# A Relu tile on ScalarE, a second query and key stack filled in the preparation, and one F32 product for the gated mixing

## The reference

```python
# layer 0: 16 heads of 16 columns; hidden width 1024
h = layernorm(x + multihead(x, x, x, sa_wq, sa_wk, sa_wv, sa_wo, causal=True), ln1_g, ln1_b)
h = layernorm(h + multihead(h, ctx, ctx, ca_wq, ca_wk, ca_wv, ca_wo, causal=False), ln2_g, ln2_b)
ff = relu(h @ ff_w1.T + ff_b1) @ ff_w2.T + ff_b2
x = layernorm(h + ff, ln3_g, ln3_b)
# layer 1: single-head gated attention over the context
qp, kp, vp = x @ Wq + bq, ctx @ Wk + bk, ctx @ Wv + bv
w = softmax(einsum('bqd,bkd->bqk', qp, kp) / 16)
y = einsum('bqk,bkd->bqd', w, vp)
gate = concatenate((qp, y), -1) @ Wg + bg
out = y * mask[..., None] * sigmoid(gate) + x
```

## Time and profile before

| | us |
|---|---|
| median of 3 runs | 853.6 (849.36 to 855.4) |
| the profiled execution | 848.75 |
| its span, first to last instruction | 846.9 |
| mean granted TensorE clock | 0.970 |

### The profile page before, as it was taken

One profiled execution on the slowest core, in us unless ns is written; L12 is line 12 of the kernel. 1 busy time (PEld: TensorE's weight loads), 2 busy tenths in 40 slices (PEclk: granted clock), 3 DMA queues, 4 the chain that ended last, 5 costly groups with the idle time before them and its releaser, 6 DMA issues.

```text
span 846.9 us, 20003 instructions
## 1 busy us (share of the span) xinstructions
PE 772.9 (91%) x7214; PEld 644.0 (76%) x7232; DVE 637.9 (75%) x1389; ACT 483.3 (57%) x1113; POOL 486.8 (57%) x598
## 2 busy tenths in 40 slices
PE   6998799999999999788899999899999899999795
PEld 5786588788877766555568888788877789889685
DVE  4535577788788898868778888987787679877854
ACT  5432256655565566565776666566656765544442
POOL 2413367776777676554355666566555677666541
PEclk9999999999999999898799999999999999999977
DMA  9675987788677664354322222222200020112122
GB/s 278 165 265 157 177 141 131 149 135 139 110 130 136 102 103 112 75 126 92 69 54 55 55 54 54 55 54 55 54 2 10 2 71 9 32 58 78 56 83 78
DMA packets 105308, 79.63 MB, mean 94 GB/s; under 512 B 43261, under 2 KB 101967, under 8 KB 104947
## 3 DMA queue, kind: packets, MB, share of 16 engines
q1 hardware_dynamic: 101850, 74.17, 41.7%
q10 hardware_dynamic: 3360, 4.18, 1.5%
HBM read 27.03 MB, written 12.97 MB: 47 GB/s over the span
## 4 chain that ended last, share of the span: by engine, by line
PE 61%; DVE 16%; issue 6%; ACT 4%; SPq 2%; DMA 1%; POOL 1%; POOLq 0%; ACTq 0%; DVEq 0%
PE a_misc L89 12%; PE a_pair L89 11%; PE a_s L1041 8%; PE a_s L806 4%; PE a_pair L830 4%; PE a_pair L848 3%; PE a_pair L1002 3%; PE a_s L804 3%; PE a_pair L987 3%; PE a_pair L1140 2%; PE a_s L964 2%; PE a_s L89 2%; DVE c_z L1593 2%; DVE a_nm L1483 2%; PE a_pair L851 1%
## 5 line engine op out<-in xcount | busy, mean ns | idle before, releaser
L1483 DVE TENSOR_REDUCE a_nm<-a_s 128x2 f32<-128x512 f32 (+1 forms) x192 | 127.1, 678 | 50.9 <-PE a_s L806 50.4
L2005 POOL TENSOR_TENSOR c_hidden<-c_hid,c_hidden 128x256 fp32r<-128x256 f32 x128 | 96.0, 750 | 109.6 <-DVE c_hid L1734 109.5
L1207 ACT ACTIVATE a_pT<-a_pair 128x512 f32<-128x512 f32 x192 | 113.6, 597 | 79.3 <-PE a_pair L830 71.6
L1337 ACT ACTIVATE a_pT<-a_pair 77x512 f32<-77x512 f32 x128 | 75.6, 591 | 100.8 <-PE a_pair L987 98.0
L1041 PE MATMUL a_s<-c_w,c_hidden 128*128 128x256 f32 x768 | 117.3, 292 | 0.0
L89 PE MATMUL a_pair<-c_fxh,c_w 128*128 128x256 f32 x512 | 100.9, 289 | 8.6 <-DVE c_hid L1734 8.5
L1912 POOL TENSOR_SCALAR_AFFINE_SELECT a_pT<-a_pT 128x256 f32<-128x256 f32 (+1 forms) x192 | 91.5, 496 | 22.4 <-ACT a_pT L1207 21.9
L1734 DVE TENSOR_SCALAR c_hid<-a_pair,ff_b_col 128x256 f32<-128x256 f32 x128 | 61.4, 479 | 51.0 <-ACT c_hidden L1363 50.6
L1041 PEld LDWEIGHTS a_s<-c_w,c_hidden 128*128 128x128 f32 x768 | 98.6, 190 | 0.6 <-issue 0.4
L89 PEld LDWEIGHTS a_pair<-c_fxh,c_w 128*128 128x128 f32 x512 | 79.1, 191 | 11.5 <-DVE c_hid L1734 11.1
L806 PE MATMUL a_s<-a_sk,a_sq 96*128 96x256 bf16 (+1 forms) x512 | 74.4, 247 | 6.9 <-DMA a_sk<-a_parts 4.4
(11 more groups left out here) (273 smaller groups left out, 2175.2 us busy)
## 6 DMA issues: line engine op xcount, KB each, us to landing
a_sq<-a_parts SPq DMA_DIRECT2D x96, 128.0 KB, 4.4
a_sk<-a_parts SPq DMA_DIRECT2D x96, 128.0 KB, 4.6
a_sq<-c_parts SPq DMA_DIRECT2D x96, 128.0 KB
x<-in_xT SPq DMA_DIRECT2D x16, 256.0 KB, 6.2
res<-in_x SPq DMA_DIRECT2D x16, 256.0 KB, 5.8
out<-g_fin SPq DMA_DIRECT2D x16, 256.0 KB, 2.1
a_sk<-kc_parts SPq DMA_DIRECT2D x96, 38.5 KB
fold_rows<-x_fold ACTq DMA_DIRECT2D x1, 2496.0 KB, 10.0
```

The costliest lines, as they stand in the source:

```text
L1207: nc.scalar.activation(pT[g % NPT][:], stps[g % 2][:], ACT.Exp).then_inc(s_exp, 1)
L1337: nc.scalar.activation(pT[g % NPX][0:SC], st_ps[0:SC, :], ACT.Exp).then_inc(c_exp, 1)
L1483: nc.vector.tensor_reduce(nm[c % 2][:, QT * heads[0] + qt:QT * heads[-1] + qt + 1:QT], sps[g % 2][:].rearrange("p (h k) -> p h k", h=len(h ...
L2005: nc.gpsimd.tensor_tensor(hl(m), hid[n % NHID][:], f32(hh(m)), ALU.subtract).then_inc(c_hl, 1)
```

## The change

- **Relu tile.** `hidden` moves from VectorE to ScalarE and reads the PSUM tile first; it frees the PSUM buffer. `hidden_high` becomes a copy of that SBUF tile to F32R and stands last in ScalarE's slot. `hidden_low` waits for the copy.
- **Second stack.** The stack of sample 1 is filled in the preparation: after the stores of each of the first six token tiles SyncE issues two of its transfers. The main stage starts with the stack of sample 2. The context keys' parts in the preparation now lie in the memory of the second stack and its neighbour, so the first of the new transfers waits until they have been stored.
- **Biases.** The column biases are loaded before the inputs, and the products that need them wait for them alone. The bias row is no longer split.
- **Mixing.** `mix` makes one F32 product for each row tile, of unsplit probabilities (now two buffers) and unsplit values, which are loaded straight to their place. `p_low`, `value_high` and `value_low` are gone. A value load waits for the mixing three samples before.

```diff
-    t.first_stack = [sb(n, [KX, H, S], BF16) for n in ("sq0", "sk0")]
+    t.first_stacks = [[sb(f"{n}{i}", [KX, H, S], BF16) for n in ("sq", "sk")] for i in range(2)]
...
-    parts = sb("parts", [P, 3, B, KT, SC], BF16)
+    parts = nc.alloc_sbuf_tensor_at("x_parts", [P, 3, B, KT, SC], BF16, offset=t.place["a_sq1"])
...
+            for n, v in t.cols.items():
+                sp.dma_start(v[:], a[n + "_col"]).then_inc(biases, 16)
             for i in range(2):
                 sp.dma_start(t.x[i][:], a["xT"][i].rearrange("(k p) s -> p k s", p=P)).then_inc(t.x_loaded[i], 16)
             for n, v in t.rows.items():
                 sp.dma_start(v[:], A(n).partition_broadcast(P)).then_inc(small, 16)
-            for n, v in t.cols.items():
-                sp.dma_start(v[:], a[n + "_col"]).then_inc(small, 16)
...
+            def load_rows(c, rows, term, i):
+                q, k = t.first_stacks[c]
+                sp.dma_start(q[rows].rearrange("r h s -> r (h s)"),
+                             t.parts[c][:, 0, term].rearrange("p k s -> p (k s)")).then_inc(t.stacked[c], 16)
+                sp.dma_start(k[rows].rearrange("r h s -> r (h s)"),
+                             t.parts[c][:, 1, i].rearrange("p k s -> p (k s)")).then_inc(t.stacked[c], 16)
+
             sp.wait_ge(t.s_p3, 1)
             for rows, term, i in stack_rows():
...
+                load_rows(0, rows, term, i)
+            sp.wait_ge(s_rowb, 1)
+            sp.dma_start(d.row, rowf[:]).then_inc(row_stored, 16)
...
                 sp.dma_start(d.vc[i * P:i * P + r], vs[i % NRING][0:r]).then_inc(t.value_stored[i % NRING], 16)
+                if i == 0:
+                    sp.wait_ge(t.s_p3, 2)
+                    sp.wait_ge(k_stored, 16)
+                if i < NTERM:
+                    load_rows(1, *list(stack_rows())[i])
...
-            pe.wait_ge(small, 16 * (len(t.rows) + len(t.cols) + 1 + 2))
+            pe.wait_ge(biases, 16 * (len(t.cols) + 2))
...
-            act.wait_ge(s_rowb, 1)
-            nc.scalar.activation(row[:, 0, :], rowf[:], ACT.Copy).then_inc(s_rowh, 1)
...
-            dve.wait_ge(s_rowh, 1)
-            nc.vector.tensor_tensor(row[:, 1, :], rowf[:], f32(row[:, 0, :]), ALU.subtract).then_inc(s_rowl, 1)
...
-    gvv = [gat(f"vv{i}", [SCE, 2, 2 * D], F32R, *p) for i, p in enumerate((("a_sq0", 0), ("a_sq0", half), ("a_sq1", 0)))]
-    raw_vv = [gat(f"raw_vv{i}", [SC, 2 * D], F32, f"a_pT{i}") for i in range(ND)]
+    gvv = [gat(f"vv{i}", [SCE, 2 * D], F32, *p) for i, p in enumerate((("a_sq0", 0), ("a_sq0", half), ("a_sq1", 0)))]
...
-    pth, ptl = (gat(n, [SCE, QT, P], F32R, "a_xl0", i * 4 * QT * P) for i, n in enumerate(("pth", "ptl")))
+    p_turned = [gat(f"pt{i}", [SCE, QT, P], F32, "a_xl0", i * 4 * QT * P) for i in range(2)]
...
-            for c in range(1, EARLY):
+            for c in range(2, EARLY):
                 load_stacks(c)
...
-                if c == 0:
-                    sp.wait_ge(c_av, 4 * B)
                 if c >= ND:
-                    sp.wait_ge(g_vl, c - ND + 1)
-                sp.dma_start(raw_vv[c % ND][:], d.vv[c * SC:(c + 1) * SC]).then_inc(g_value[c % ND], 16)
+                    sp.wait_ge(g_xo, c - ND + 1)
+                sp.dma_start(gvv[c % ND][0:SC], d.vv[c * SC:(c + 1) * SC]).then_inc(g_value[c % ND], 16)
...
-                pe.wait_ge(g_ptl, c + 1)
-                pe.wait_ge(g_vl, c + 1)
+                pe.wait_ge(g_pth, c + 1)
+                pe.wait_ge(g_value[c % ND], 16 * (c // ND + 1))
                 for qt in range(QT):
-                    for i, (x, y) in enumerate(((0, 0), (1, 0), (0, 1))):
-                        last = mt(xo(c)[:, qt * 2 * D:(qt + 1) * 2 * D], (pth, ptl)[x][:, qt, :], gvv[c % ND][:, y, :], start=False, stop=i == 2,
-                                  skip_group_check=True)
+                    last = mt(xo(c)[:, qt * 2 * D:(qt + 1) * 2 * D], p_turned[c % 2][:, qt, :], gvv[c % ND][:], start=False, stop=True,
+                              skip_group_check=True)
...
+            def hidden(n):
+                c, m = divmod(n, FT)
+                if not real(c):
+                    return
+                act.wait_ge(c_up, n + 1)
+                atleast(act, c_hl, n - NHID + 1)
+                nc.scalar.activation(hid[n % NHID][:], up[n % 2][:, 0:S], ACT.Relu, bias=b1[:, m:m + 1]).then_inc(c_hid, 1)
+
             def hidden_high(n):
...
-                act.wait_ge(c_up, n + 1)
+                act.wait_ge(c_hid, n + 1)
                 atleast(act, c_down, n - FT + 1)
-                nc.scalar.activation(hh(m), up[n % 2][:, 0:S], ACT.Relu, bias=b1[:, m:m + 1]).then_inc(c_hh, 1)
+                nc.scalar.activation(hh(m), hid[n % NHID][:], ACT.Copy).then_inc(c_hh, 1)
...
-            def p_high(c):
+            def p_copy(c):
...
-                atleast(act, g_xo, c)
-                nc.scalar.activation(pth[:], pt[0:SCE, 0:S].rearrange("p (q s) -> p q s", q=QT), ACT.Copy).then_inc(g_pth, 1)
+                atleast(act, g_xo, c - 1)
+                nc.scalar.activation(p_turned[c % 2][:], pt[0:SCE, 0:S].rearrange("p (q s) -> p q s", q=QT), ACT.Copy).then_inc(g_pth, 1)
...
-                nc.scalar.activation(gvv[c % ND][0:SC, 0, :], raw_vv[c % ND][:], ACT.Copy).then_inc(g_vh, 1)
...
-                nc.vector.tensor_scalar(hid[n % NHID][:], up[n % 2][:, 0:S], b1[:, m:m + 1], 0.0, ALU.add, ALU.max).then_inc(c_hid, 1)
...
-                nc.vector.tensor_tensor(ptl[:], pt[0:SCE, 0:S].rearrange("p (q s) -> p q s", q=QT), f32(pth[:]), ALU.subtract).then_inc(g_ptl, 1)
...
-                pool.wait_ge(c_hid, n + 1)
+                pool.wait_ge(c_hh, n + 1)
...
-                nc.gpsimd.tensor_tensor(gvv[c % ND][0:SC, 1, :], raw_vv[c % ND][:], f32(gvv[c % ND][0:SC, 0, :]), ALU.subtract).then_inc(g_vl, 1)
```

More of the change, by code:

```diff
@@ L145, in context_products @@
     bgr, bvr = sb("bgr", [1, D], F32), sb("bvr", [1, D], F32)
-    rowf, row = sb("rowf", [1, 2 * D], F32), sb("row", [1, 2, 2 * D], F32R)
+    rowf = sb("rowf", [1, 2 * D], F32)
     cb0 = sb("cb0", [1, 1], F32)
@@ L530, in causal_cross_feed_gated @@
     xh, xl, parts, rest = t.xh, t.xl, t.parts, t.rest
-    sq, sk = ([first] + [sb(f"{n}{i}", [KX, H, S], BF16) for i in range(1, NSTK)] for first, n in zip(t.first_stack, ("sq", "sk")))
+    sq, sk = ([first, second] + [sb(f"{n}{i}", [KX, H, S], BF16) for i in range(2, NSTK)]
+              for first, second, n in zip(*t.first_stacks, ("sq", "sk")))
     vpad = [sb(f"vpad{i}", [P, QT, H, 2 * DH], F32) for i in range(NVP)]
@@ L629, in causal_cross_feed_gated @@
     stored = [sem("out_stored") for _ in range(2)]
-    names = ("nmr", "half", "onef", "one", "pad", "z", "zg", "h", "ht", "xh", "xl", "sc", "max", "exp", "rec", "p", "pt", "pth", "ptl",
-             "gates", "xo", "fact", "gated", "fin", "vh", "vl", "zero", "blank")
-    (g_nmr, g_half, g_onef, g_one, g_pad, g_z, g_zg, g_h, g_ht, g_xh, g_xl, g_sc, g_max, g_exp, g_rec, g_p, g_pt, g_pth, g_ptl,
-     g_gates, g_xo, g_fact, g_gated, g_fin, g_vh, g_vl, g_zero, g_blank) = (sem("g_" + n) for n in names)
+    names = ("nmr", "half", "onef", "one", "pad", "z", "zg", "h", "ht", "xh", "xl", "sc", "max", "exp", "rec", "p", "pt", "pth",
+             "gates", "xo", "fact", "gated", "fin", "zero", "blank")
+    (g_nmr, g_half, g_onef, g_one, g_pad, g_z, g_zg, g_h, g_ht, g_xh, g_xl, g_sc, g_max, g_exp, g_rec, g_p, g_pt, g_pth,
+     g_gates, g_xo, g_fact, g_gated, g_fin, g_zero, g_blank) = (sem("g_" + n) for n in names)
     real = lambda b: 0 <= b < B
@@ L2121, in program @@
         d.wqg = nc.dram_tensor("wqg_parts", (P, 2 * KT * D), F32).ap()
-        d.row = nc.dram_tensor("bias_row", (1, 4 * D), F32).ap()
+        d.row = nc.dram_tensor("bias_row", (1, 2 * D), F32).ap()
         d.cb = nc.dram_tensor("key_bias", (1, B * 2 * SCE), F32).ap()
```

58 lines of the change are left out of this document (14 added, 44 removed).

## The result

The changed kernel takes 830.2 us (median, 828.1 to 832.0) against 853.9 us before: ratio 0.973, 95% interval 0.969 to 0.977, a gain of 23.7 us. I had forecast 843.4 us with a range from 834 to 852. The direction was right, the gain more than twice the forecast, and the time lies outside the range. A second measurement further down, on another chip, gives 0.9765 (0.974 to 0.979). The profiled execution took 831.0 us, its span is 828.6 us; before it was 848.75 and 846.9.

The account below looks back on a forecast made before the run. TensorE, busy 91% of the span, was taken as the bound. Terms -5.8 - 7.5 + 6.3 - 2.1 - 1.1 gave -10.2 us: 838.6 us profiled, 843.4 us as median; the forecast's own range was 839 to 848, overall 834 to 852.

Parts of the forecast that it names:

- The start, -5.8: Main stage's start: TensorE's 4.4 us wait for stack 1 and 1.4 us from late x of sample 4 vanish.
- The preparation's end, 0: Preparation: the twelve moved transfers fit SyncE's free time, and earlier biases and the unsplit bias row end no notable wait: 0.
- The Relu tile, -7.5: Feed-forward: up-tile and output-projection waits, ceiling 12.9 us, give 9 us; less 1.5 for ScalarE's copies; bounds 0 and -12.9.
- 1.5 us for ScalarE's burst: Thin stretch near 673.85 us: ScalarE's added copies delay TensorE in four samples by 0.35 to 0.4 us each, +1.5.
- The gated mixing, +6.3 - 2.1 - 1.1: Gated stage: F32 products cost +6.3 us; the last value-split wait (-2.1) and one collision near 799 us (-1.1) go.
- Freed VectorE time buys nothing: Rival, chance 0.17: waits on line 1734 become equally long waits for maxima or exponentials; sum -2.7, 850.9 us.
- the preparation pays: Rival, chance 0.11: moved transfers delay the preparation's stores or early loads and the 5.8 us come back; sum -4.4, 849.2 us.
- ScalarE as the pacer: Rival, chance 0.12: copies in three burst slots of all 16 samples reach TensorE, 19.2 us; sum +16.5, 870.1 us.
- Everything is won: Rival, chance 0.12: all 12.9 us of Relu-related waits go and mixing takes 1.65 us; about -17, 836.6 us.
- One sign of being wrong: Profile after: ScalarE's exponentials appearing as the releaser of over 6 us of TensorE's waits would show the forecast wrong.

Follow-up runs that it names:

- The two kernels with old instructions kept: Kernel before with F32 mixing alone, plus unread old instructions: GpSimd's value subtraction with ScalarE's copy, 0.9987; or VectorE's subtraction for the probabilities' low part, 0.9899.
- the second copy: Changed kernel with a second copy of each Relu tile on ScalarE, 128 more: ratio 0.9783 against the kernel before.
- the probe: Kernel before with only the Relu tile moved, plus an unread VectorE statistics instruction over 128x256 at the old place, waiting for ScalarE's Relu: 1.0113 against before.

## Why the prediction was right or wrong

**The start, -5.8: right.** The part alone gave 5.0 us (3.0 to 7.1), though in its one profile the lead grows by only 2.7 us from 60 to 120 us: the granted clock is at its low level there for 10 us from 77.6 us on, in the changed kernel's profile not at all. In the changed kernel's profile the lead grows by 6.3 us from 80 to 110 us. SyncE's queue, in order of time:

```profile
73.87 0.56 SPq L709 DMA_DIRECT2D a_sq<-a_parts  x1
...
83.78 0.47 SPq L701 DMA_DIRECT2D x<-in_xT  x1
```

x of sample 4 leaves 9.5 us earlier than in the earlier trace rows, 7.7 were expected, and ScalarE no longer waits for it (2.32 us in the earlier trace rows). The lead grew by what the two waits were worth.

**The preparation's end, 0: right for the moved transfers, wrong for the biases.** It ended 1.4 us earlier. The step "the earlier column biases and the missing split of the bias row end no wait of over 0.4 us on TensorE: 0" read the profile before, in which slow products at the start hid the wait. Two products of 462 columns, first before, then after:

```profile
10.80 0.97 PE L89 MATMUL x_k<-x_ctx_high,x_cwk 128*128 128x462 f32 x2
```

```profile
10.54 0.58 PE L89 MATMUL x_k<-x_ctx_high,x_cwk 128*128 128x462 f32 x2
```

Before, they took twice as long from start to start until 13.8 us, after only until about 8.5. The trace's records of the granted clock begin just there, at its high level: at 13.76 and at 8.50 us; in front of that there is no record, so the low level is read from the doubled times. Over all profiles the records begin between 7.5 and 16.2 us: by 8.9 us in all seven kernels that load the biases first and in five of the ten others. But in those five the main stage starts 1.4 to 2.4 us later than before: TensorE waits 1.1 to 1.6 us for the last small load, and its granted clock falls for 3.4 us behind that wait. With the biases first this wait arises in none of the seven. Why the clock rises when it does stays open. The moved transfers cost at most 0.6 us: with the stack part alone the main stage's first transfer is at 75.86 us, before at 75.30.

**The Relu tile, -7.5: right in size, wrong in its reason.** It gave 7.7 us. The copy, taken at 0.40 us, took 0.41. The 1.5 us for ScalarE's burst came as worked out: the waits for the cross exponentials behind 433 us went from 1.1 to 2.6 us. But the step "the PSUM buffer of an up tile is now released after the Relu on ScalarE" is not why it pays: with the release early and an instruction of the same size still in VectorE's queue, nothing was won. I had counted 61.4 us of VectorE's work as gone and then looked only at who waited for that instruction.

**The gated mixing, +6.3 - 2.1 - 1.1: this is the step that failed.** The F32 price was right (0.33 us a sample, taken at 0.35; 16 of them are 5.3 us), the wait of 2.1 us did go. The failed step is the sentence that the splits that go "lie beside TensorE's work, except in two places". GpSimd's subtraction, 16 times 1.28 us, was priced at -3.2 us (the last wait, -2.1, and one collision, -1.1) and was worth -10.2. The row that told it stood in the earlier trace rows, a two-element step of 1.25 us, and I read it as one accident near 799 us instead of asking how often VectorE's short steps take over a microsecond. The sum with that one term mended (-10.2 instead of -1.1 and -2.1) is -17.2 us; the four parts measured together gave 23. The biases are 1.7 of the rest, and most of what is left, 3.9, lies in what the F32 mixing gives back besides: with it the changes alone came to -8.8 and not to -10.2 + 5.3 = -4.9. In its profile the granted clock is at the low level for 9 us in all behind 435 us, before for 24, and a mixing product of 0.59 us takes 1.06 at that level. The two kernels with old instructions kept have 6 and 11 us there, but the changed kernel, F32 as well, has 18 in both of its profiles. Whether the low clock follows from the products' form stays open.

**The rivals.** "Freed VectorE time buys nothing" is refuted by the Relu tile's 7.7 us, and "the preparation pays" by the 0.6 us above. ScalarE as the pacer, the one on the other side, is refuted by the second copy. Its rule, relu on VectorE (the Trainium skill, "ScalarE: Activation LUTs", section "Rules for kernel authors"), speaks of the engine's own speed; here the move won 7.7 us, with VectorE at 75% and ScalarE at 57% busy before, and the Relu itself took 479 ns on VectorE and 464 on ScalarE. "Everything is won" named 836.6 us and was still short, because its ceiling was the sum of waits with the names of the changed tiles on them. One sign of being wrong was badly chosen: exponentials release 7.8 us of TensorE's waits over the whole span, more than the 6 named, but they released 7.2 before already.

**What went against the change and was not foreseen.** The stretch from 380 to 420 us gave 5.0 us back in the profiled runs. Busy time and granted clock (the column behind the five engines) of the same stretch, before, then changed, then with the stack part alone, then with the mixing part alone:

```profile
330.00:430.00 100.00, 81.13 (x824) 54.89 (x823) 80.32 (x174) 64.43 (x140) 47.24 (x61) 0.88 0.39 86
```

```profile
330.00:430.00 100.00, 82.93 (x785) 55.90 (x774) 75.52 (x165) 60.09 (x134) 44.32 (x55) 0.80 0.40 84
```

```profile
330.00:430.00 100.00, 79.98 (x815) 53.55 (x805) 80.31 (x171) 62.65 (x137) 47.87 (x61) 0.88 0.42 87
```

```profile
330.00:430.00 100.00, 82.72 (x792) 55.22 (x784) 77.38 (x166) 60.10 (x130) 46.63 (x61) 0.81 0.39 86
```

The stack part, which moves the stretch by 2.5 us, left the clock at 0.88. The mixing part changes no instruction between the preparation and 640 us and still had 0.81. Two kernels with the old mixing and one other edit, also behind 640 us, had 24 and 27 us of low clock from 310 to 435 us, before 24; the F32 mixing alone had 38, and with an old instruction kept 27 and 41. So kernels alike up to there differ by up to 17 us, and no single part is shown to be at work. With the whole change it was 41 us in both profiles; whether that is chance stays open.

The profiled pair differs by 17.7 us and the medians by 23.7, because the profiled execution of before was 5.1 us faster than its median and that of the changed kernel 0.9 slower.

## What to carry over

A short instruction on a lightly used GpSimd can cost more than its length on the critical path: look through VectorE's rows for steps of a few elements that take a microsecond, and see which GpSimd instruction ends with them, before pricing any GpSimd work at nothing. And when work leaves a crowded engine, count the time that everything behind it in the queue gains, not only the waits that carry the moved tile's name. An instruction kept with an unread result tells in one run whether its place in the queue counts; the probe must be held up by what held the original and by nothing else, and it brings back the original's wait along with its time. And a term put at nothing because the profile shows no wait deserves a second profile: here slow products at the start had hidden one.

## What the hardware showed that I had not expected

VectorE's additions, products and scalings that read SBUF alone stop for what is left of a running GpSimd instruction (0.17 us becomes 1.14, 0.42 us becomes up to 1.5), down to steps over two numbers a partition. Those that read PSUM (0.48 us), the reciprocals (0.25 us in line 1699) and the statistics instruction (0.43 us at most) are not held in the trace of before, nor the last in the probe's. An unread addition of 128x256 at 128 places put the kernel 45 us above before; an unread statistics instruction there, 9.6. And TensorE left its low level at the start anywhere between 7.5 and 16.2 us.
